# A perceiver layer on one core: the experts' start moved into the self-attention program, the third norm in two groups, the first tile's rows by selection products

## The reference

```python
x = x + xattn(layernorm(x), ctx_1024, Wq, bq, Wkv, bkv, Wproj, bproj)   # 8 x 1601 context rows
x = x + attn(layernorm(x), WQ, WK, WV_down, WV_up)                      # 16 heads, diagonal of the softmax
x = x + ffn(layernorm(x), Wg, bg, W1, b1, W2, b2)                       # experts, the best 2 of 8 per row

def moe_forward(x, Wg, bg, W1, b1, W2, b2):
    gates = softmax(x @ Wg + bg)
    mask = one_hot(top_k(gates, 2)).sum(-2)
    g = gates * mask;  g = g / max(sum(abs(g)), 1e-12)
    h = gelu(x @ W1[e] + b1[e])                # 512 -> 2048, for each expert e
    return sum_e(g[e] * (h @ W2[e] + b2[e]))   # 2048 -> 512
```

## Time and profile before

| | us |
|---|---|
| Median of 3 runs | 1457.33 |
| Lowest and highest | 1456.17, 1459.87 |
| The profiled execution | 1458.49 |
| its span | 1456.7 |
| TensorE busy | 1333.2 (92%) |
| VectorE busy | 943.2 (65%) |
| ScalarE busy | 763.7 (52%) |
| GpSimd busy | 108.3 (7%) |

### The profile page before, as it was taken

The page is one execution under the profiler, slowest core; times in us unless marked ns, Lnnn a source line. Parts: engine busy times, 40 slices in busy tenths (PEclk is TensorE's granted clock), DMA queues, the critical chain, the costliest instruction groups (busy, mean ns, idle before and its releaser), DMA issues. The chain is left out here.

```text
span 1456.7 us, 21925 instructions
## 1 busy us (share of the span) xinstructions
PE 1333.2 (92%) x7367; PEld 1158.2 (80%) x7368; DVE 943.2 (65%) x1494; ACT 763.7 (52%) x1326; POOL 108.3 (7%) x78
## 2 busy tenths in 40 slices
PE   5999999999999999999999999857999279999995
PEld 4788888888898899889889889745887167877774
DVE  3666666666567667667666666557776736487872
ACT  3455555565565556556556555443331346477761
POOL 0000000000000000000000000365311400000002
PEclk9999999999999999999999999968999689999998
DMA  5221011011110110111112112553370657399983
GB/s 187 76 66 29 27 44 50 26 43 43 32 43 22 53 43 22 37 31 51 29 32 58 29 32 43 108 142 65 59 288 1 222 210 240 105 358 338 340 293 101
DMA packets 129586, 146.39 MB, mean 100 GB/s; under 512 B 66424, under 2 KB 69880, under 8 KB 129536
## 3 DMA queue, kind: packets, MB, share of 16 engines
q1 hardware_dynamic: 128272, 141.75, 31.6%
q0 software_dynamic: 1280, 4.20, 0.9%
HBM read 125.28 MB, written 20.12 MB: 100 GB/s over the span
## 5 line engine op out<-in xcount | busy, mean ns | idle before, releaser
L543 DVE SCALAR_TENSOR_TENSOR Ks<-ps_scores,bkc,Ks 64x384 fp32r<-64x384 f32 (+2 forms) x254 | 160.5, 632 | 147.1 <-ACT Ks L428 144.6
L166 PE MATMUL ps_scores<-cT_hi,Wkv_hi 128*128 128x384 f32 (+2 forms) x508 | 184.4, 363 | 6.4 <-DVE Wkv_lo L565 6.4
L506 ACT ACTIVATE Pr<-ps_scores,stat 128x705 f32<-128x705 f32 (+1 forms) x128 | 119.5, 933 | 115.5 <-DVE stat L633 115.5
L168 PE MATMUL ps_scores<-cT_hi,Wkv_lo 128*128 128x384 f32 (+2 forms) x508 | 175.2, 345 | 0.0
L167 PE MATMUL ps_scores<-cT_lo,Wkv_hi 128*128 128x384 f32 (+2 forms) x508 | 174.7, 344 | 0.0
L428 ACT ACTIVATE Ks<-ps_scores,bkc 64x384 fp32r<-64x384 f32 (+2 forms) x254 | 149.4, 588 | 42.5 <-PE ps_scores L168 40.7
L166 PE MATMUL ps_scores<-Wkv_hi,cT_hi 128*128 128x512 f32 (+1 forms) x412 | 170.1, 413 | 0.4 <-DVE Ks L543 0.4
L493 ACT CAST PT<-ps_turn 128x512 fp32r<-128x512 f32 (+2 forms) x256 | 110.2, 483 | 110.5 <-PE ps_turn L778 109.7
L549 DVE TENSOR_TENSOR Vs<-ps_scores,Vs 128x512 fp32r<-128x512 f32 (+1 forms) x103 | 71.2, 691 | 149.0 <-ACT Vs L432 148.3
L168 PE MATMUL ps_scores<-Wkv_hi,cT_lo 128*128 128x512 f32 (+1 forms) x412 | 161.8, 393 | 0.0
L167 PE MATMUL ps_scores<-Wkv_lo,cT_hi 128*128 128x512 f32 (+1 forms) x412 | 161.1, 391 | 0.0
(11 more groups left out here) (344 smaller groups left out, 2494.2 us busy)
## 6 DMA issues: line engine op xcount, KB each, us to landing
wu_raw<-in_L_ffn_W_dram SPq DMA_DIRECT2D x64, 1024.0 KB, 7.6
raw<-in_ctx_dram SPq DMA_DIRECT2D x16, 768.0 KB, 4.6
raw<-in_ctx_dram SPq DMA_DIRECT2D x8, 1024.0 KB, 5.2
raw<-in_ctx_dram SPq DMA_DIRECT2D x8, 512.0 KB
sorted_x<-zeros SPq DMA_DIRECT2D x1, 4096.0 KB, 14.8
sorted_out<-zeros SPq DMA_DIRECT2D x1, 4096.0 KB, 26.0
o_heads<-U SPq DMA_DIRECT2D x56, 64.0 KB, 1.7
oA<-o_heads SPq DMA_DIRECT2D x8, 448.0 KB, 9.1
```

Source lines behind the costliest of these rows:

```text
L166: nc.tensor.matmul(out_ap, sh, mh, start=(i == 0), stop=False)
L168: last = nc.tensor.matmul(out_ap, sl, mh, start=False, stop=(i == len(pairs) - 1))
L506: nc.scalar.activation(Pr[:, i % 2, 0:VALID[c]], S_cols(c, 0, VALID[c]), ACT.Exp, bias=stat[:, 0, c, i:i + 1], accum_out=stat[:, 1, c, i:i ...
L543: ins = nc.vector.scalar_tensor_tensor(out=Ks[c][64:128, j, o:o + wide], in0=acc[64 * h:64 * h + 64, 0:wide], scalar=bkc[:, j:j + 1], in1= ...
```

## The change

One program instead of two. The expert part of each engine becomes a function (`sync_experts`, `pool_experts`, `scalar_experts`, `vector_experts`, `tensor_experts`), which is called behind that of self-attention, and some of it is moved ahead:

- Units 0 to 3 of expert 0 are loaded once the last values matmul is made. Unit 0 is split between the second softmax and the last `vT` splits, units 1 and 2 before the last sums, unit 3 behind the turned third norm. Unit 4 is loaded and copied before the norm, too.
- The third norm has two groups: tiles 0 to 2 (each tile's sum directly ahead of its statistics), then tile 3. The second norm has that form already.
- Tile 0's rows no longer come back from HBM. `sel[:, t, j]` is 1 where the place of row t * 128 + p is j (`row_no` holds 0 to 127), and the product of `xn3` and `sel`, summed over the four `t`, gives the rows of tile 0 turned. The place of the higher expert isn't looked at, since tile 0 holds rows of expert 0 only. The eight indirect writes stay, for the other tiles.
- `xn3` moves to the top of SBUF. `xg`, `b2row` and `eo` share its place, so the loads of `b2row` and of tile 1's rows wait for the scatter and the selection; the loads of units 2 and 3 of expert 1 stand behind them on SyncE.
- The constants and the zeros of `b1rows` are made during self-attention.

The core of the diff; the functions' bodies not shown are the old ones, indented less.

```diff
--- before.py
+++ after.py
-        def norm_vector(dve, n, x, xn, tmp, tiles=range(TT)):
+        def norm_vector(dve, n, x, xn, tmp, tiles=range(TT), prepare=None, between=None):
             for t in tiles:
+                if prepare:
+                    prepare(t)
                 ins = nc.vector.bn_stats(stats[:, t, :], x[:, t, :])
...
+            if between:
+                between()
             dve.wait_ge(sem("ln_root"), n)
...
             exp_diagonal(1)
+            first_weights_hi(act, 0)
             for j in range(HP):
                 v_hi_of(1, j)
...
             values_of(1)
+            first_weights_lo(dve, 0)
             for j in range(HP):
                 v_lo_of(1, j)
             dve.wait_ge(sem("x_doubled"), 1)
-            for t in range(TT):
-                dve.wait_ge(sem("up_made"), t + 1)
-                nc.vector.tensor_tensor(x_sum[:, t, :], x_sum[:, t, :], bank(t), ALU.add).then_inc(sem("x_2"), 1)
...
+        xn3 = sb(LATE + 106496, "xn3", [P, TT, D])
+        kept = area(LATE + 106496, LATE + 114688)
+        xg = kept("xg", [P, D])
+        b2row = kept("b2row", [P, D])
+        eo = kept("eo", [P, D])
+        row_no = kept("row_no", [P, 1, P])
+        sel = kept("sel", [P, TT, P])
-        xn3 = sb(LATE + 73728, "xn3", [P, TT, D])
+        V_MADE, V_DONE = USE_V[1] + TT, USE_V[1] + TT
...
+        def first_weights_hi(act, v):
+            act.wait_ge(sem(f"wu_in{v}"), 16)
+            if v >= RING + 2:
+                act.wait_ge(sem("up_made"), TT)
+            nc.scalar.copy(wu_hi[v][:, :, :], wu_raw[v % RING][:, :, :]).then_inc(sem("wu_hi_done"), 1)
...
+            sp.wait_ge(sem("b_made"), V_MADE)
             for v in range(RING):
                 load_unit(0, v)
-            load_b2(0)
+            sp.wait_ge(sem("b_done"), V_DONE)
+            sp.wait_ge(sem("sorted_zeroed"), 32)
...
+            load_next(1, 0)
+            load_next(1, 1)
+            sp.wait_ge(sem("x_sorted"), 16 * 2 * TT)
+            sp.wait_ge(sem("g_turned"), 1)
+            load_b2(0)
+            sp.wait_ge(sem("table_ready"), 1)
+            load_next(1, 2)
+            load_next(1, 3)
...
+            pool.wait_ge(sem("up_made"), 1)
+            nc.gpsimd.memset(f32(b1rows[:, :]), 0.0).then_inc(sem("b1rows_zeroed"), 1)
...
+            for v in range(1, RING):
+                first_weights_hi(act, v)
+            act.wait_ge(sem("up_made"), 1)
             nc.scalar.activation(ones_r[:, :], ident[:, :], ACT.Copy, bias=1.0, scale=0.0).then_inc(sem("ones_r"), 1)
-            turn_scalar(act, x3T_hi)
+            first_weights_hi(act, 4)
+            norm_scalar(act, 4, lnt3, FIRST_TILES)
+            turned_hi(0)
+            turned_hi(1)
+            norm_scalar(act, 5, lnt3, LAST_TILE)
+            turned_hi(2)
+            turned_hi(3)
+            act.wait_ge(sem("x_turned"), KC + 1)
+            nc.scalar.copy(x3T_hi[:, :, LAST], psS[:, :, LAST]).then_inc(sem("x_turned_hi"), 1)
...
+            first_weights_lo(dve, 1)
+            first_weights_lo(dve, 2)
+            norm_vector(dve, 4, x_sum, xn3, lnt3, FIRST_TILES, prepare=sum_in, between=lambda: second_sum(TT - 1))
+            norm_vector(dve, 5, x_sum, xn3, lnt3, LAST_TILE)
+            first_turned()
...
+            first_weights_lo(dve, 3)
...
             ts(place[:, 0, :], ends[:, 0, :], FAR, None, ALU.add).then_inc(sem("placed"), 1)
+            link(ts(col[:, :], ends[:, 0, :], FAR, None, ALU.add))
+            for t in range(TT):
+                ins = ts(sel[:, t, :], row_no[:, 0, :], col[:, t:t + 1], None, ALU.is_equal)
+            ins.then_inc(sem("first_selected"), 1)
...
+            first_weights_lo(dve, 4)
+            first_weights_lo(dve, 5)
+            gathered_lo(0)
...
+            first_weights_lo(dve, 6)
             dve.wait_ge(sem("b1_out"), 32)
-            dve.wait_ge(sem("x_sorted"), 16 * 2 * TT)
+            first_weights_lo(dve, 7)
...
-            pe.wait_ge(sem("table_ready"), 1)
-            turn_gathered(0)
+            pe.wait_ge(sem("first_selected"), 1)
+            for k in range(KC):
+                for t in range(TT):
+                    ins = nc.tensor.matmul(bank(6)[:, k * P:(k + 1) * P], xn3[:, t, k * P:(k + 1) * P],
+                                           sel[:, t, :], start=(t == 0), stop=(t == TT - 1))
+            ins.then_inc(sem("g_turned"), 1)
+            pe.wait_ge(sem("table_ready"), 1)
```

767 lines of the change are left out of this document (380 added, 387 removed).

## The result

| | before | after |
|---|---|---|
| median of the runs, us | 1457.88 (1456.17 to 1459.87, 4 runs) | 1442.38 (1440.39 to 1444.41, 4 runs) |
| profiled execution, us (span) | 1458.49 (1456.7) | 1441.31 (1439.4) |

The medians differ by 15.5 us and the profiled executions by 17.2, where 18.8 were predicted. The ratio, 0.9874 with a 95% interval of 0.985 to 0.9899, is not the quotient of these two medians (0.9894): taken of 1457.88 us it is a gain of 18.4 us, 14.7 to 21.9. So the gain is 15.5 us by the medians of four runs each and about 18 by the rest, and these times can't settle a difference of 2 us. The account therefore goes by the profiles.

What follows compares the result with a forecast made beforehand. TensorE, busy 92% of the span, was taken as the bound, so only its idle time pays. Gains of 1.8 + 15.2 + 1.8 = 18.8 us off the median 1457.33 gave 1438.5 us, range 1434.5 to 1446.

Steps and rivals of the forecast that it cites:

- Step 1: Self-attention: early loading and splitting of expert 0's first units costs near nothing, hidden behind TensorE's matmuls.
- Rival (d): Self-attention: unit 0 lands late, ScalarE stops ahead of `vT_hi`, and the kernel is slower, 1466.0 us; chance 0.02.
- step 4: Start of the experts: making tile 0's rows by selection instead of from HBM gains 15.2 us, bounds 9.5 and 17.7.
- Step 2: Third norm, after self-attention's last sum: two groups instead of one gain 1.8 us, bounds 0.6 and 3.0.
- Step 3: Gating chain, from the logits' end to `place`: no change in length.
- (a): Selection products: each pass bound by its weight load at low clock, 10.6 us instead of 5.5, 1443.6 in all; chance 0.09.
- (b): Selection comparisons: VectorE blocked by GpSimd's first indirect write, up to 3.1 us, 1441.6 in all; chance 0.05.
- Step 5: Tile 0's first 4.6 us, formerly at low clock: the products ahead raise the clock, gain 1.8 us, bounds 0 and 2.2.
- Step 6: Expert tiles: no change, with margins of 2 us in tile 0 and 3 us for tile 1's `xg`.
- Rival (c): Tile 0: the gain is partly given back as tile 1's `xg` or unit 7 is 4 us late, 1442.5; chance 0.10.

Runs made afterwards that it cites:

- the late splits: Changed kernel with the splits of expert 0's units 0 to 4 put behind the gating: 1456.4 us, 0.9969; with bias rows loaded first as well, 1455.57 us, 0.9959.
- the fillers: Changed kernel with 18 useless matmuls in TensorE's gating gaps and `gT_lo` ahead of unit 5's subtraction: 1440.82 us, ratio 0.9872 to the kernel before.
- the standard of the last group: Changed kernel with the next expert's bias rows loaded ahead of its last weight unit, run once more: 1440.68 us, ratio 0.986 to the kernel before.
- the repetition: Changed kernel run again without an edit, beside the kernel before: 1442.07 us, ratio 0.9877.

## Why the prediction came out as it did

**Step 1, the weights: right.** ScalarE waits for no unit ahead of the turned values: unit 0 was copied, and then ScalarE waited 4.00 us for TensorE.
```profile
1107.11 1.91 ACT L1575 CAST wu_hi<-wu_raw 128x2048 fp32r<-128x2048 f32 x1
1113.01 1.74 ACT L1240 CAST vT_hi<-ps_turn 128x512 fp32r<-128x512 f32 x3 [4.00 <-PE ps_turn L1432]
```
The last sum starts no later than before (1129.5 to 1131.2 in all executions, with these splits and without, but for two at 1135.2 and 1135.4). Rival (d) had nothing to stand on: the unit landed within 6 us of its issue at 1101.1. What the prediction didn't say is what the late splits showed, that this step carries step 4.

**Step 2, the norm: right in its size, 1.83 us against 1.8,** but 1.1 of it come from the statistics between the sums and the missing block entry, and 0.73 from the two groups, half of which or more the products take back. One term of the clock was wrong without harm: TensorE had not fallen to the low clock after its 3.2 us without work. The granted clock was 1.00 from 1132.87 to 1133.87, with the transposes begun at 1132.99, and 0.52 in the next us; it rose again near 1140.7, 10.9 us after the last sum's start, where the sum had 10.6.

**Step 3, the gating: right.** From the logits' end to `place` 6.5 us both times (1148.20 - 1141.70, and 1150.85 - 1144.37).

**Step 4, the selection: 14.4 us against 15.2.** What is left of 16.2 after the 1.83 of step 2. The comparisons took 0.87 (0.75 forecast), and the products 6.28 (5.5): this is the term that was mis-sized. I had let the low clock end after 4 us. It lasted until about 5.2: over the 2.3 us behind the first 4 the granted clock was 0.74, which is 1.2 us of the low level and 1.1 of the full one. At 0.22 and 0.12 us a pass that makes 24 passes and 8, 6.2 us. In the prediction's terms 4 us made 18 passes. At the full clock from the start, as with the fillers, 32 take 3.84 us, 0.12 each, so the price of a pass (0.11) was right. Rivals (a) and (b) are both refused: no pass waits for a weight load of its own (the loads take 0.33 us at the low clock and 0.19 at the full one, beside passes 0.22 and 0.12 apart), and VectorE's four comparisons take 0.87 us while GpSimd begins its first write at 1148.49.
```profile
1148.30 0.87 DVE L1863 TENSOR_SCALAR sel<-row_no,col 128x128 f32<-128x128 f32 x4
```
```profile
1148.49 1.17 POOL L1677 DMA_INDIRECT sorted_x<-xn,place  x1 [25.15 <-DVE place L1860]
1149.97 3.05 POOL L1677 DMA_INDIRECT sorted_x<-xn,place  x1 [0.30 <-issue]
```
The rule of the Trainium skill that I weighed there (SBUF — State Buffer, Who interferes with whom) did not cost VectorE anything: here again only GpSimd was slowed, 3.05 us for the write that ran beside VectorE's subtraction of a unit, 0.96 for one alone. The same section of the Trainium skill says of such a subtraction, with both inputs in SBUF, that it contends with a GpSimd instruction that reads SBUF, which the prediction left out. The slowed writes are in line with it; that it is their reading of the places that waits is not shown.

**Step 5, the clock in tile 0: 2.1 us against 1.8.** The tile took 25.66 us against 27.80, all of it at 1.00. Steps 4 and 5 together thus gained 16.5 of 17.0: products at the low clock are paid once, and tile 0 doesn't pay again.

**Step 6, the tiles unchanged: this step failed.** 18.35 us of the 18.8 stand at tile 1, and 1.9 and 1.8 are lost from there to the end in the two executions of the changed kernel. The prediction said that from there on every load hangs on TensorE's own progress as before. But the bias rows' load hangs on the load ahead of it, and that one on VectorE: the waits for `b1rows` grew from 3.1 us to 5.5 and 4.4. How that became a loss differs. In the first profile the waits for `h_lo` fell by as much, and the loss is the stretch at the low clock behind one stop of 2.24 us (1.5 us). In the second all waits together grew from 6.9 to 8.5 us. With the bias rows early in both kernels, 0.2 to 0.4 us of 1.7 are left up to the last matmul. What that rest is stays open; two executions of one kernel differ there by 0.1 to 0.2 us.

Rival (c), the gain given back in tile 0 by `xg` of tile 1, was not true, but near: a start 2.4 us earlier was enough for TensorE to wait for it. The margin that I had put at 3 us was 2.1 in the changed kernel (the load was issued at 1170.06, was 7.2 us on its way, and TensorE turned the rows at 1179.36), and 1.7 in the standard of the last group.

How near the 18.8 was is not known to a us. The profiles say 17.2 in all and 16.5 from the last sum on, the first medians 15.5, the ratio 18.4, and the repetition 18.0 and 18.9. The single executions of each kernel spread over 3.7 and 4.0 us at first, and over 6.8 each in the repetition. The sum was right up to tile 1 (18.35), with a clock term 0.8 us short in step 4 and 0.3 us to the good in step 5; that it also agrees with the times, though the tiles gave back 1.8 us beside the profile before, is in part luck.

## What to carry to other kernels

When a wait is removed from the start of a long bound stretch, ask of each load inside that stretch what stands ahead of it in its queue and what that waits for: the 16 KB load was issued only when the 1 MB load ahead of it could be, and that was when VectorE was done. Put small things that are ready first. An edit that was put at no gain of its own may be what makes the other edit pay; undo it under the full change before calling it free or useless. A second gain behind the first (here the fillers' 2.4 us) has to be followed to the end, since the next late thing, `xg`, was within 2.1 us, and 2.4 us are less than these times can tell. And compare all waits of a stretch, and its busy time, not only the wait that grew: here another one shrank by as much, and the loss was in the clock.
